# Single-unit expert loads put ahead of the two-unit loads, and the last rows transposed inside the down product before them, in a one-core fp32 decoder layer

## The chip, the cores and the metric

One core of one Trainium2 chip runs the whole program. The metric is the device time in microseconds (us) of one execution, as the median of several; lower is better.

## The reference, cut to what matters

A pre-norm decoder layer on x of 8 x 112 rows of 512 (896 rows): causal attention with 16 heads of 128, cross attention with 32 heads of 16 over 375 context rows per batch, then a mixture of experts. The change touches the last part alone:

```python
probs = softmax(x @ gate_w.T); w, sel = top_k(probs, 2); w /= w.sum()
combine = sum(one_hot(sel, 8) * w[..., None], axis=1)              # 896 x 8
out = silu(x @ shared_gate.T) * (x @ shared_up.T) @ shared_down.T   # inner size 704
y = einsum('nei,ehi->neh', silu(g) * u, expert_down)               # 8 experts, inner size 352
out = out + einsum('neh,ne->nh', y, combine)
x = x + out
```

## The kernel before, in words

The rows that go to one expert are gathered into slots of 128, called units. 21 units always suffice for 896 x 2 choices over 8 experts, and so 21 are computed (`NBLK`, L23). An expert's weights are loaded either for two units (kind "p", seven such loads) or for one (kind "o", seven). The list `jobs` (L324) holds the order of the loads: three shared ones ("s", numbers k = 0 to 2), then p, o, p, o ... to number 16. `its` (L326 to L335) is the list of the steps: one per shared load and one per unit, so 3 + 21. Two weight buffers exist of each kind: `F` (as loaded, fp32) and `E` (its split into a high and a low part, fp32r); load k uses number k % 2.

Each product in fp32 is made of three matmuls on high and low parts (`mm3`, L511). So each loaded weight has to be split: ScalarE writes the high part (`part_hi`, L1234), VectorE subtracts to get the low part (`part_low`, L1645). A routed load is split in four pieces: 0, 1 and 2 for the up and gate weights, 3 for the down weights. `splits(n, when)` (L376 to L387) says which pieces are split in step n: `when` 0 is at the step's start, 1 is at its end. In the pattern of before, pieces 0 to 2 of a two-unit load are split in the step of the one-unit load ahead of it, and pieces 0 to 2 of a one-unit load in the first of the two steps of the two-unit load ahead of it. For the first routed load (k = 3) all three pieces of load 4 come at the end of the step (L386).

TensorE's step for a unit (`job_pe`, L874) is: gate product of unit j (`expert_up(j, 0)`, 12 matmuls), transpose of the previous unit's hidden rows (`turn_h`, 3), transpose of the next unit's rows (`turn_x`, 4), up product (`expert_up(j, 1)`, 12), down product of the previous unit (`job_down`, 9). In the first routed step the down product of the last shared load stands second, and none stands at the end. `expert_up` waits for all three up pieces of its load. After the last step come `turn_h` and `job_down` of the last unit, unit 20 (L958, L959).

VectorE's step (`job_dve`, L1677) is: the splits of `when` 0, the low part of the previous unit's transposed hidden rows (`ht_low_dve`), the low part of the next unit's transposed rows, the product silu(g) * u (L1710), the splits of `when` 1, and `y_out` of the previous unit: its down product times the routing weight, from PSUM to `yg` (L1667). ScalarE goes in the same order (`job_act`, L1266), with the high part of the hidden rows (`ht_hi_act`) and the silu. Each engine works in the order in which its program stands.

GpSimd adds each unit's rows to the output in HBM with an indirect DMA (`add_back`, L2005). Units of one load have no row in common. Units of different loads can have, and so `add_back` waits until all adds of the load before have landed, but not for an add of its own load (L2009 to L2012).

SyncE issues the loads. `part_load(k, 0)` brings the up and gate weights (1408 KB), `part_load(k, 3)` the down weights (768 KB); each waits until VectorE has split the same pieces of load k - 2. The loop at L2174 sets the order of the queue, with one `xg_load` (the rows of the unit four later) per step.

Of the kernel before, what the change touches and what calls it, by code (L numbers as in the profile page):

```python
# [12 lines left out]
NB, T, D, NT = 8, 112, 512, 896  # L13
# [9 lines left out]
NBLK = (2 * NT + NE * (BS - 1)) // BS  # L23
NP, NO = 7, 7
NSL = NP + NO
RW = D + 2
IC = ((0, 128), (128, 128), (256, 96))
WU = KC * 2 * NI
# [52 lines left out]
def decoder_layer(nc, x_d, ctx_d, wqk_d, wv_d, wo_d, wqx_d, wkv_d, gw_d, moe_d, wexp_d, ident_d, mask_d, cst_d,  # L81
                  out_d):
    stack = ExitStack()
    with stack:
# [131 lines left out]
        o = wide + WE * 4  # L216
# [3 lines left out]
        o = end_a  # L220
# [6 lines left out]
        o = place_w + 2 * SC * 4  # L227
# [29 lines left out]
        small, o, o2 = {}, start_p, wide + WE * 4 + 2 * SC * 4  # L257
# [28 lines left out]
        for n, u in enumerate(pj_uses):  # L286
            if n == pj_turn:
                kb_last = pj_last[0], pj_last[1]
            i = n % 4 + (2 if n >= pj_turn else 0) if n + 1 < len(pj_uses) else 6
# [28 lines left out]
        for n, u in enumerate(tx_uses):  # L318
            i = 3 if n >= tx_turn else 7
# [1 line left out]
        KB, SX, AB = banks[0:2], banks[2:6], banks[6]  # L321


        jobs = [("s", j) for j in range(3)] + [(kd, q) for q in range(NP) for kd in "po"]  # L324
        NJ = len(jobs)
        its, unit_of, job_of, last_of = [], [], [], {}  # L326
        for k, (kd, q) in enumerate(jobs):
# [21 lines left out]
        for n, (kind, j, k, _) in enumerate(its):  # L349
            prev = its[n - 1] if n else None  # L350
# [17 lines left out]
        for n, u in enumerate(ups):  # L368
            i = gb[n]
# [6 lines left out]
        def splits(n, when):  # L376

            kind, j, k, second = its[n]
            if kind == "s":
                return ([(1, 0), (1, 3)], [(2, 0), (2, 3)], {0: [(3, 0)], 2: [(3, 1), (3, 2)], 1: [(3, 3)]}.get(when))[k] if when == 2 or k == 2 else []  # L380
            if when == 2 or k == NJ - 1 and not second:
                return []
            if second:
                return ([(k, 3)] if k > 3 else [], [(k + 1, 3)])[when]
            if k == 3:
                return [(4, 0), (4, 1), (4, 2)] if when else []  # L386
            return ([(k + 1, 0), (k + 1, 1)], [(k + 1, 2)])[when]  # L387
# [14 lines left out]
        for b in range(NB):  # L402
            r, row_parts[b] = 0, []
            while r < T:
                j, p = (b * T + r) // 128, (b * T + r) % 128
# [102 lines left out]
        def tensor(e):  # L508
# [96 lines left out]
            for j in range(NA + 2):  # L605
                if 1 <= j <= NA:
                    i = j - 1
# [217 lines left out]
            def turn_h(j):  # L825
                u = ("h", j)
                w.wait_ge(*gu_dve["b", j])
                t_wait(u)
                for k, (o, n) in enumerate(IC):
                    i = e.transpose(TB[u][0:n, k * 128:(k + 1) * 128], (hh1 if j % 2 else hh[0])[:, o:o + n], ident[:, :])  # L830
                i.then_inc(*t_full.did(u))
# [16 lines left out]
                else:  # L848
                    w.wait_ge(*y_done[v])

            def job_down(kind, j):
                k = job_of[j] if kind == "e" else at_job[kind, j]
                p = E[k % 2]
                if kind == "e":
                    u = (kind, j)
                    part_wait(k, 3)
                    w.wait_ge(*ht_lo[j])
                    y_wait(u)
                    for i, (o, n) in enumerate(IC):
                        z = WU + i * D  # L860
                        t = mm3(YB[u][:, :], (hT[j % 2][0][0:n, i, :], hT[j % 2][1][0:n, i, :]),
                                (p[0][0:n, z:z + D], p[1][0:n, z:z + D]), i == 0, i == 2)
                    t.then_inc(*y_full.did(u))
                    return
                w.wait_ge(*h_lo[1, 2 * j + 1])
                for t in range(4):
                    u = (kind, j, t)
                    y_wait(u)
                    for q in range(2):
                        i = mm3(YB[u][0:T, :], at(hs1 if q else hs[0], ALL, toks(t * T, T)), at(p, ALL, toks((WU if q else 0) + 1024, D)),  # L870
                                q == 0, q == 1)
                    i.then_inc(*y_full.did(u))

            def job_pe(n):  # L874
                kind, j, k, _ = its[n]
                prev = its[n - 1][0:2] if n else None
                nxt = its[n + 1] if n + 1 < len(its) else (None, 0)
                if kind == "e":
                    expert_up(j, 0)
                else:  # L880
                    up_pe(1, 2 * j, 0)
                if prev and prev[0] == "e":
                    turn_h(prev[1])
                elif prev and kind == "e":
                    job_down(*prev)
                if kind == "s":
                    up_pe(1, 2 * j, 1)
                    if k == 0:
                        up_pe(1, 2 * j + 1, 0)
                if nxt[0] == "e":  # L890
                    turn_x(nxt[1])
                if kind == "e":
                    expert_up(j, 1)
                if prev and (prev[0] == "e" or kind == "s"):
                    job_down(*prev)
                if kind == "s":
                    if k:
                        up_pe(1, 2 * j + 1, 0)
                    up_pe(1, 2 * j + 1, 1)
# [55 lines left out]

            for n in range(len(its)):
                job_pe(n)
            turn_h(NBLK - 1)  # L958
            job_down("e", NBLK - 1)  # L959


# [401 lines left out]
        def vector(e):  # L1363
# [91 lines left out]
            for j in range(NA + 2):  # L1455
# [7 lines left out]
                if 1 <= j <= NA:  # L1463
                    i = j - 1
# [191 lines left out]
            def ht_low_dve(j):  # L1656
                w.wait_ge(*ht_hi[j])
                low(hT[j % 2][1][:, :, :], TB["h", j][:, 0:3 * BS].rearrange("p (k t) -> p k t", k=3), hT[j % 2][0][:, :, :]).then_inc(
                    *ht_lo.did(j))

            def y_out(kind, j):
                if kind == "e":
                    w.wait_ge(*y_full[kind, j])
                    w.wait_ge(*meta_in[0])
                    if j > 3:
                        w.wait_ge(*added[j % 4][j - 4])
                    e.tensor_scalar(yg[j % 4][:, :], YB[kind, j][:, :], meta[:, unit_of[j], 1:2], None, ALU.mult).then_inc(  # L1667
                        *y_done.did((kind, j)))
                    return
                for t in range(4):  # L1670
                    u = (kind, j, t)
                    w.wait_ge(*y_full[u])
                    if j:
                        w.wait_ge(*y_done[kind, j - 1, t])
                    e.tensor_tensor(xs[:, 4 + t, :], xs[:, 4 + t, :], YB[u][0:T, :], ALU.add).then_inc(*y_done.did(u))

            def job_dve(n):  # L1677
                kind, j, k, _ = its[n]
                prev = its[n - 1] if n else (None, 0)
                nxt = its[n + 1] if n + 1 < len(its) else (None, 0)  # L1680
                if kind == "s":
                    up_mul(1, 2 * j)
                    for i in splits(n, 0):
                        part_low(*i)
                    if k:
                        y_out(*prev[0:2])
                    up_low(1, 2 * j)
                    if nxt[0] == "e":
                        turned_low(nxt[1])
                    for i in splits(n, 2):  # L1690
                        part_low(*i)
                    up_mul(1, 2 * j + 1)
                    up_low(1, 2 * j + 1)
                    for i in splits(n, 1):
                        part_low(*i)
                    return
                if prev[0] == "s":
                    y_out(*prev[0:2])
                for i in splits(n, 0):
                    part_low(*i)  # L1700
                if prev[0] == "e":
                    ht_low_dve(prev[1])
                if nxt[0] == "e":
                    turned_low(nxt[1])
                if j > 1:
                    w.wait_ge(*t_full["h", j - 2])
                u = ("b", j, 1)
                w.wait_ge(*gu_act["b", j])
                w.wait_ge(*gu_full[u])
                e.tensor_tensor((hh1 if j % 2 else hh[0])[:, 0:NI], (sg1 if j % 2 else sg[0])[:, 0:NI], GU[u][:, 0:NI],  # L1710
                                ALU.mult).then_inc(*gu_dve.did(("b", j)))
                for i in splits(n, 1):
                    part_low(*i)
                if prev[0] == "e":
                    y_out(*prev[0:2])

            def wqx_low(k):
# [186 lines left out]
            for n in range(len(its)):  # L1904
                job_dve(n)
            ht_low_dve(NBLK - 1)
            y_out("e", NBLK - 1)


# [115 lines left out]
        def sync(e):  # L2025
# [146 lines left out]
            part_load(4, 0)  # L2172
            part_load(4, 3)
            for kind, j, k, second in its[3:]:  # L2174
                if jobs[k][0] == "p":
                    part_load(k + 3 if second else k + 2, 0)
                else:
                    part_load(k + 1, 3)
                    part_load(k + 2, 3)
                xg_load(j + 4)  # L2180
                if j == 0:
                    for b in range(4, NB):
                        store(b)
# [67 lines left out]
```

## Time and profile before

| what | value |
| --- | --- |
| median of 3 runs | 963.21 us (962.73 to 963.60) |
| the profiled execution's own time | 963.22 us |
| its span in the trace | 961.4 us |
| TensorE busy | 928.0 us, 97% of the span |
| VectorE, ScalarE, GpSimd busy | 544.2, 455.5, 178.3 us |
| DMA | 94.12 MB, 98 GB/s over the span |

How to read it: PE is TensorE, PEld its weight load, DVE VectorE, ACT ScalarE, POOL GpSimd, SP SyncE (SPq its queue). Rows give microseconds from the start of the span. Time before the span and behind it is 1.8 us in the profiled execution. "L1367" is the line of the helper that makes every low part, "L966" the one that makes every high part, "L512" to "L514" are the three matmuls of `mm3`, "L830" is `turn_h` and "L822" `turn_x`.

### The profile page before, as it was taken

How to read it: one execution, taken by the hardware profiler on the slowest of the kernel's cores; microseconds unless marked ns; L12 is line 12 of the kernel's file. 1: busy time of each engine (PE TensorE's matmuls, PEld its weight loads, DVE VectorE, ACT ScalarE, POOL GpSimd, SP SyncE). 2: the span in 40 equal slices, each digit the busy share in tenths (PEclk: the TensorE clock that was granted, in tenths of full speed). 3: DMA queues.
4: the chain of work that ended last, by engine and by line, in shares of the span. 5: the costliest groups of instructions: out<-in, count | busy, mean ns of one | idle time of the engine just before them, and what ended most of it. 6: DMA issues, size and time to landing. Idle time of an engine off the chain costs nothing.

```text
span 961.4 us, 17906 instructions
## 1 busy us (share of the span) xinstructions
PE 928.0 (97%) x7250; PEld 807.5 (84%) x7250; DVE 544.2 (57%) x1192; ACT 455.5 (47%) x1113; POOL 178.3 (19%) x137
## 2 busy tenths in 40 slices
PE   4999999999999999999999999999999999999995
PEld 3999999999999999877777777777778888999994
DVE  6254444444444445485645546555457766888882
ACT  3342323232323233446666666566575234665651
POOL 1220202020202022411011011011000710223232
PEclk9999999999999999999999999999999999999998
DMA  5210442020202003212110010010032685998973
GB/s 190 67 45 22 166 164 66 24 66 22 66 23 67 22 22 110 65 47 88 55 34 23 13 34 23 13 33 13 1 125 80 231 247 185 335 301 280 303 198 44
DMA packets 31329, 94.12 MB, mean 98 GB/s; under 512 B 6176, under 2 KB 9488, under 8 KB 29328
## 3 DMA queue, kind: packets, MB, share of 16 engines
q1 hardware_dynamic: 26944, 83.80, 25.6%
q0 software_dynamic: 4304, 9.19, 4.7%
q8 instruction: 57, 0.93, 0.4%
q14 instruction: 24, 0.20, 0.1%
HBM read 74.33 MB, written 16.81 MB: 95 GB/s over the span
## 4 chain that ended last, share of the span: by engine, by line
PE 90%; DVE 5%; ACT 2%; issue 1%; DMA 1%; SPq 0%; POOL 0%; DVEq 0%
PE bank L512 25%; PE bank L513 24%; PE bank L514 24%; PE bank L709 3%; PE bank L726 3%; PE bank L559 3%; PE bank L584 3%; PE bank L676 1%; PE bank L571 1%; PE bank L822 1%; PE bank L736 1%; PE bank L600 1%; PE bank L830 1%; DMA wqk_f<-wqk 1%; DVE kT L1528 1%
## 5 line engine op out<-in xcount | busy, mean ns | idle before, releaser
L1130 ACT ACTIVATE ee<-bank 125x448 f32<-125x448 f32 x192 | 91.0, 547 | 22.0 <-PE bank L709 21.0
L512 PE MATMUL bank<-xT_hi,wqk_hi 128*128 128x448 f32 x256 | 95.9, 375 | 1.4 <-DVE xT_lo L1367 1.4
L514 PE MATMUL bank<-xT_lo,wqk_hi 128*128 128x448 f32 x256 | 93.8, 366 | 0.0
L513 PE MATMUL bank<-xT_hi,wqk_lo 128*128 128x448 f32 x256 | 93.6, 365 | 0.0
L512 PE MATMUL bank<-wkv_hi,ctx_hi 128*125 128x512 f32 x192 | 80.3, 418 | 2.6 <-DVE kn L1519 2.0
L1367 DVE TENSOR_TENSOR E_lo<-F,E_hi 128x940 fp32r<-128x940 f32 (+2 forms) x62 | 81.0, 1330 | 2.4 <-ACT E_hi L966 2.3
L513 PE MATMUL bank<-wkv_hi,ctx_lo 128*125 128x512 f32 x192 | 76.1, 396 | 0.0
L514 PE MATMUL bank<-wkv_lo,ctx_hi 128*125 128x512 f32 x192 | 75.7, 394 | 0.0
L512 PE MATMUL bank<-wv_hi,xT_hi 128*112 128x256 f32 x256 | 72.2, 282 | 0.0
L513 PE MATMUL bank<-wv_hi,xT_lo 128*112 128x256 f32 x256 | 71.8, 280 | 0.0
L514 PE MATMUL bank<-wv_lo,xT_hi 128*112 128x256 f32 x256 | 71.7, 280 | 0.0
L1914 POOL TENSOR_TENSOR ctx_lo<-ctx_f,ctx_hi 128x500 fp32r<-128x500 f32 x24 | 30.4, 1267 | 220.4 <-ACT ctx_hi L966 220.4
L1449 DVE TENSOR_TENSOR xa<-xa,bank 128x512 f32<-128x512 f32 x56 | 38.4, 686 | 53.1 <-PE bank L514 53.1
L966 ACT ACTIVATE E_hi<-F 128x940 fp32r<-128x940 f32 (+2 forms) x62 | 68.0, 1146 | 0.9
L1528 DVE COPY kT<-bank 128x250 f32<-128x250 f32 x48 | 20.0, 418 | 84.8 <-PE bank L676 84.7
L2016 POOL DMA_INDIRECT out<-yg,meta x21 | 38.8, 1849 | 142.9 <-DVE yg L1667 76.8
L1914 POOL TENSOR_TENSOR wqk_lo<-wqk_f,wqk_hi 128x1024 fp32r<-128x1024 f32 x16 | 37.8, 2362 | 145.4 <-ACT wqk_hi L966 145.4
L966 ACT ACTIVATE qk<-bank 128x448 f32<-128x448 f32 x32 | 17.4, 545 | 96.1 <-PE bank L514 96.1
L1025 ACT ACTIVATE pp<-sm,nm 112x112 f32<-112x112 f32 x128 | 48.0, 377 | 30.7 <-DVE nm L1421 30.7
L512 PE MATMUL bank<-E_hi,xgT_hi 128*128 128x352 f32 x168 | 56.3, 335 | 0.0
L1110 ACT ACTIVATE sq<-bank 125x256 f32<-125x256 f32 (+1 forms) x64 | 24.6, 384 | 64.6 <-PE bank L514 64.6
L514 PE MATMUL bank<-E_lo,xgT_hi 128*128 128x352 f32 x168 | 54.2, 322 | 0.0
(323 smaller groups left out, 2401.0 us busy)
## 6 DMA issues: line engine op xcount, KB each, us to landing
F<-wexp SPq DMA_DIRECT2D x14, 1408.0 KB, 7.4
F<-wexp SPq DMA_DIRECT2D x14, 768.0 KB
wqk_f<-wqk SPq DMA_DIRECT2D x16, 512.0 KB, 3.4
ctx_f<-ctx SPq DMA_DIRECT2D x24, 250.0 KB, 2.7
slots<-zt SPq DMA_DIRECT2D x1, 5397.0 KB, 19.0
xg<-slots SPq DMA_DIRECT2D x21, 256.0 KB, 7.0
F<-moe SPq DMA_DIRECT2D x6, 768.0 KB, 6.8
wv_f<-wv SPq DMA_DIRECT2D x8, 512.0 KB, 3.6
```

The costliest lines, as they stand in the source:

```text
L512: e.matmul(out, a[0], b[0], start=first, stop=False)
L513: e.matmul(out, a[1], b[0], start=False, stop=False)
L514: return e.matmul(out, a[0], b[1], start=False, stop=last)
L559: i = e.matmul(banks[4 + g][0:T, c * T:(c + 1) * T], q[:, 0, toks(b * T, T)], q[:, 1, toks(b * T, T)], start=True, stop=True)
L966: return e.activation(out, src, ACT.Copy)
L1025: i = e.activation(pp[g][:, c, :], sm[g][:, c, :], ACT.Exp, bias=nm[g][:, c:c + 1], scale=ISQ, accum_out=rs[g][:, c:c + 1])
L1130: e.activation(ee[(4 * n + r) % 8][:, :], SX[r][0:MS, 0:4 * T], ACT.Exp, scale=0.25).then_inc(*x_exped.did((n, r)))
L1367: return e.tensor_tensor(out, src, high.bitcast(F32), ALU.subtract)
L1449: e.tensor_tensor(xa[:, j, :], xa[:, j, :], PJ[u][:, :], ALU.add).then_inc(*pj_dve.did(u))
L1528: e.tensor_copy(kT[n % 6][:, :, :], TX["t", (u, m)][:, 0:2 * MS].rearrange("p (g t) -> p g t", g=2)).then_inc(*k_copied.did((u, m)))
L1914: return e.tensor_tensor(out, src, high.bitcast(F32), ALU.subtract)
L2016: e.indirect_dma_start(out_d, bass.IndirectOffsetOnAxis(ap=meta[:, unit_of[j], 0:1].bitcast(U32), axis=0), yg[j % 4][:, :], None, compute_ ...
```

## The change

The list of loads alternates o, p instead of p, o. So the routed loads begin with a one-unit load (k = 3) and end with a two-unit load (k = 16); unit numbers and the work per unit stay. `splits` and SyncE's order of loads follow. The last step now makes the first third of unit 19's down product, transposes unit 20's hidden rows, and then makes the other two thirds. `y_out` of unit 19 goes behind the low part of unit 20's hidden rows.

```diff
-        jobs = [("s", j) for j in range(3)] + [(kd, q) for q in range(NP) for kd in "po"]
+        jobs = [("s", j) for j in range(3)] + [(kd, q) for q in range(NP) for kd in "op"]
...
             if second:
-                return ([(k, 3)] if k > 3 else [], [(k + 1, 3)])[when]
+                return ([(k, 3)], [(k + 1, 3)] if k + 1 < NJ else [])[when]
             if k == 3:
                 return [(4, 0), (4, 1), (4, 2)] if when else []
...
-            def job_down(kind, j):
+            def job_down(kind, j, inner=range(3)):
...
-                    for i, (o, n) in enumerate(IC):
-                        z = WU + i * D
+                    for i in inner:
+                        n, z = IC[i][1], WU + i * D
                         t = mm3(YB[u][:, :], (hT[j % 2][0][0:n, i, :], hT[j % 2][1][0:n, i, :]),
                                 (p[0][0:n, z:z + D], p[1][0:n, z:z + D]), i == 0, i == 2)
-                    t.then_inc(*y_full.did(u))
+                    if i == 2:
+                        t.then_inc(*y_full.did(u))
...
-                if prev and (prev[0] == "e" or kind == "s"):
+                if n == len(its) - 1:
+                    job_down(*prev, (0,))
+                    turn_h(j)
+                    job_down(*prev, (1, 2))
+                elif prev and (prev[0] == "e" or kind == "s"):
                     job_down(*prev)
...
             for n in range(len(its)):
                 job_pe(n)
-            turn_h(NBLK - 1)
             job_down("e", NBLK - 1)
...
-                if prev[0] == "e":
+                if prev[0] == "e" and n + 1 < len(its):
                     y_out(*prev[0:2])
...
             ht_low_dve(NBLK - 1)
+            y_out("e", NBLK - 2)
             y_out("e", NBLK - 1)
...
             for kind, j, k, second in its[3:]:
-                if jobs[k][0] == "p":
-                    part_load(k + 3 if second else k + 2, 0)
-                else:
-                    part_load(k + 1, 3)
+                if k == 3 or jobs[k][0] == "p" and not second:
+                    part_load(k + 2, 0)
+                if second:
+                    part_load(k + 2, 3)
+                    part_load(k + 3, 0)
+                elif jobs[k][0] == "o":
                     part_load(k + 2, 3)
                 xg_load(j + 4)
```

## Rows read from the trace of the kernel before

**Rows 1.** The page: chain of work that ended last, shares by engine.

```profile
PE 90%; DVE 5%; ACT 2%; issue 1%; DMA 1%; SPq 0%; POOL 0%; DVEq 0%
```

**Rows 2.** Busy time in stretches: us, each engine's busy time, granted clock, DMA share, GB/s.

```profile
783.00:812.00 29.00, 28.79 (x141) 24.27 (x140) 18.64 (x23) 10.94 (x16) 0.00 (x0) 1.00 0.69 225
812.60:945.00 132.40, 132.40 (x791) 123.37 (x790) 109.48 (x131) 79.22 (x111) 35.74 (x19) 1.00 0.83 261
```

**Rows 3.** Timeline, first routed step's end: start, duration, engine, line, tiles, [idle before].

```profile
811.74 2.74 ACT L966 ACTIVATE E_hi<-F 128x940 fp32r<-128x940 f32 x3
...
812.52 0.33 PE L514 MATMUL bank<-E_lo,xgT_hi 128*128 128x352 f32 x1
...
812.69 0.32 PE L512 MATMUL bank<-E_hi,xgT_hi 128*128 128x352 f32 x1
...
812.96 0.52 DVE L1710 TENSOR_TENSOR sg<-sg,bank 128x352 f32<-128x352 f32 x1 [0.73 <-PE bank L514]
...
813.39 3.22 DVE L1367 TENSOR_TENSOR E_lo<-F,E_hi 128x940 fp32r<-128x940 f32 x3
```

**Rows 4.** The chain of waits, a wait of TensorE for VectorE: start, duration, what.

```profile
806.68 0.69 DVE xs L1675
...
807.42 0.49 PE bank L512
```

**Rows 5.** Timeline, around the end of a later one-unit step.

```profile
925.56 1.13 DVE L1367 TENSOR_TENSOR E_lo<-F,E_hi 128x936 fp32r<-128x936 f32 x1
...
926.87 0.19 PEld L512 LDWEIGHTS bank<-E_hi,xgT_hi 128*128 128x128 f32 x1 [0.21 <-DVE E_lo L1367]
```

**Rows 6.** Timeline, the last step and what follows it.

```profile
944.54 0.39 PE L512 MATMUL bank<-E_hi,hT1hi 128*128 128x512 f32 x1
...
944.84 0.52 DVE L1710 TENSOR_TENSOR sg<-sg,bank 128x352 f32<-128x352 f32 x1 [0.92 <-PE bank L514]
...
946.63 0.49 PE L830 MATMUL bank<-ident,sg 128*128 128x128 f32 x3
946.83 0.75 DVE L1667 TENSOR_SCALAR yg<-bank,meta 128x512 f32<-128x512 f32 x1 [1.46 <-PE bank L514]
947.15 0.49 ACT L966 ACTIVATE hT0hi<-bank 128x384 fp32r<-128x384 f32 x1 [3.46 <-PE bank L830]
947.68 0.56 DVE L1367 TENSOR_TENSOR hT0lo<-bank,hT0hi 128x384 fp32r<-128x384 f32 x1
947.86 1.55 POOL L2016 DMA_INDIRECT out<-yg,meta  x1 [4.61 <-DVE yg L1667]
...
948.34 0.47 PE L512 MATMUL bank<-E_hi,hT0hi 128*128 128x512 f32 x1 [1.22 <-issue]
...
950.28 0.40 PE L514 MATMUL bank<-E_lo,hT0hi 96*128 96x512 f32 x1
950.72 0.75 DVE L1667 TENSOR_SCALAR yg<-bank,meta 128x512 f32<-128x512 f32 x1 [2.48 <-PE bank L514]
953.24 1.55 POOL L2016 DMA_INDIRECT out<-yg,meta  x1 [3.83 <-issue]
```

**Rows 7.** DMA issues of the stretch 946 to 961.4: tiles, count, median us to landing.

```profile
out<-yg,meta POOLq DMA_INDIRECT x2, 4.7
```

**Rows 8.** Busy time in a stretch behind the last matmul, columns as in rows 2.

```profile
954.00:955.00 1.00, 0.00 (x0) 0.00 (x0) 0.00 (x0) 0.00 (x0) 0.78 (x1) 0.72 0.00 0
```

**Rows 9.** Timeline, near the start: the same matmul at both levels of the clock.

```profile
18.64 0.72 PE L512 MATMUL bank<-xT_hi,wqk_hi 128*128 128x448 f32 x1
...
22.52 0.41 PE L513 MATMUL bank<-xT_hi,wqk_lo 128*128 128x448 f32 x1
```

**Rows 10.** Landing of the 28 issues of line 2141 (the routed loads): one line.

```profile
DMA to landing us min/median/max: 6.1/7.4/9.3
```

**Rows 11.** Timeline, SyncE's issues over a two-unit load's steps.

```profile
873.72 0.34 SPq L2141 DMA_DIRECT2D F<-wexp  x1
...
876.52 5.27 SPq L2141 DMA_DIRECT2D F<-wexp  x2
```

## The prediction

> **What bounds the kernel now.** I read the page's chain of waits first: TensorE holds 90% of it, "issue" 1%, DMA 1% [rows 1]. Then the busy time by stretch: from 812.6 to 945 us, which is all of the routed part but its first step and its last two microseconds of steps, TensorE is busy 132.40 of 132.40 us at the full granted clock, with 791 matmuls [rows 2]. A unit takes 40 matmuls (12 + 12 + 9, and 7 transposes), so a step lasts 132.4 x 40 / 791 = 6.7 us, and no wait of another engine shows in it. In the stretch before (783 to 812) TensorE lacks 0.2 us. So a reordering of the loads can't gain anything in the middle: 21 units make the same matmuls in either order. It can only open a gap where there was none, or close something at the two ends. The timeline of both ends therefore decides.
>
> **The end, before.** Unit 19's down product begins at 944.54; nine matmuls later, at 946.63, so 0.23 us for each, the transposes of unit 20 follow, ScalarE's high part starts at 947.15, VectorE's low part at 947.68, and the last down product at 948.34: TensorE idles 1.22 us. Its last matmul starts at 950.28, VectorE scales from 950.72 to 951.47, but GpSimd issues the last add only at 953.24, 3.83 us idle, since it waits for the add of 947.86 to land [rows 6]. From that issue to the end of the span are 961.4 - 953.2 = 8.2 us.
>
> **The change, part by part.** The sum is made against the profiled execution, 963.22 us, which is also the median (963.21).
>
> 1. *First routed step.* This is the part that costs. Load 4 is now needed one step earlier, since load 3 serves one unit and not two. Its three up pieces are still split at the end of step 3, behind the product silu(g) * u, and TensorE has nothing left there: the down product of the shared load stood second in that step. The rows show the whole chain. The last matmul of the step starts at 812.52, and the next unit's first at 812.69. VectorE makes the product at 812.96 and the three low parts from 813.39 on, 3.22 us in all, to 816.61; ScalarE's high parts run from 811.74 to 814.48, ahead of them [rows 3]. From a VectorE end to the matmul it releases 0.05 us pass (807.37 to 807.42) [rows 4]. So unit 1's gate product starts at 816.65 instead of 812.69: 3.96 us. The first matmul after a gap takes 0.1 to 0.25 us more (0.49 us long where others take 0.40 [rows 4]); I take 0.1. **Cost 4.1 us**, 3.9 to 4.3. Nothing takes it back, since TensorE has no later idle time to absorb it [rows 2].
>
> 2. *Later steps of one-unit loads.* There too the next load's third up piece is split at the end of the step, and the next unit needs it at once, but the down product of the previous unit covers it. The trace has this pattern six times already: the low part starts at 925.56 and takes 1.13 us, to 926.69, and TensorE's next weight load comes at 926.87 [rows 5]. Its cover is only some 0.2 us longer than it. Cost 0 as the pattern stays the same; without cover it would be up to 1.1 us each.
>
> 3. *First step of the two-unit loads, and the move of the piece-3 splits.* As many ScalarE and VectorE instructions as before, in the same kinds of steps; VectorE is busy 109.5 of 132.4 us, ScalarE 79.2 [rows 2]. In the new last step VectorE has one piece more at its start: 1536 elements where 940 take 1.07 us [rows 3], so 1.8 us. `ht_low` can't start there before the gate product's 12 matmuls, 0.17 us each [rows 3], and the transposes are done, over 2.5 us in. Cost 0.
>
> 4. *SyncE's queue.* 28 loads as before. The up part of a one-unit load now goes out behind the down part of the load ahead, so at about 876.9 instead of 873.72 [rows 11], and behind 768 KB. Two steps of 13.4 us lay between its issue and the first step that splits it; 10.2 us are left. Landing takes 6.1 to 9.3 us, median 7.4 [rows 10]; 768 KB at 261 GB/s [rows 2] are 3.0 us, but part of that is in these landings already. TensorE needs those pieces a further step later, so that only a delay of ScalarE's and VectorE's queue could matter. Cost 0, with an upper end below. `xg_load` goes out a step late at most and is needed three steps on: 0.
>
> 5. *Unit 20's transposes inside unit 19's down product.* A third of the down product, 3 x 0.23 us, ends at 945.24. `turn_h` waits for VectorE's product, 944.84 + 0.52, so it starts at about 945.45 and TensorE idles 0.2 us. The high part, low part and down product follow 0.52, 1.05 and 1.71 us behind, as before [rows 6]: 947.17. The three transposes and six matmuls fill TensorE until then. So the last down product starts 948.34 - 947.17 = 1.2 us earlier. Its scaled rows are there at 951.47 - 1.17 = 950.30, and GpSimd can issue 0.28 us later (947.58 to 947.86): 950.58.
>
> 6. *No wait between the last two adds.* `y_out` of unit 19 comes after its six later matmuls, at 947.36 to 948.10, and its add at 948.38, with 1.55 us of work, so to 949.93 [rows 6]. The last add's 950.58 is later than that, so it goes out at once, 2.66 us before the old 953.24. An add alone takes 4.7 us to land [rows 7]. Add 19 must now wait for add 18, of another load, but a whole step of 6.7 us lies between the two, and 4.7 us is what landing takes. **Gain 2.7 us** with part 5. If the two adds, 2.2 us apart, got in each other's way wholly, the second would be as if it had waited, and the end would come at 948.38 + (953.24 - 947.86) = 953.76 instead of 953.24: a loss of 0.5 us. Nearest row is the lone add; I take 2.7.
>
> Sum: 963.2 + 4.1 - 2.7 = **964.6 us**, 0.15% above before. A measurement of this kernel can tell about 0.2% from no change, so 961.3 to 965.1 counts as the same. The forecast's own range is 964.1 to 965.3.
>
> **The rivals.**
>
> *A, slower: the gap lowers TensorE's clock.* The new gap is 4.0 us long, longer than any that TensorE has while at full clock. At the end of the run the granted clock is 0.72 on average over 954 to 955 [rows 8], with levels 1.0 and 0.5, so it fell at about 954.4, 3.8 us after the last matmul ended. Near the start, ten 448-column matmuls go out from 18.64 to 22.52, 0.39 us apart, before one takes 0.41 us instead of 0.72 [rows 9]: that stretch ran at half clock. At the full one 352 columns follow after 0.17 us (812.52 to 812.69) [rows 3], which is 0.22 for 448. So a fall would cost such a stretch once, 3.9 x (1 - 0.22/0.39) = 1.7 us, and up to twice that if it stays longer: 966.3, up to 968.0. For it: the lengths are almost equal. Against it: the matmuls on either side are dense. The Trainium skill ("TensorE: Matmul & The Clock Gate", HAM oscillation) says that idle stretches between bursts of matmuls send the clock back to half rate; by that rule the time is this rival's, without it the forecast's. The fall at the end of the trace agrees, but the trace has no such gap with matmuls behind it.
>
> *B, slower: the last add gains little.* If the second add's data queue behind the first's, the end gives between -0.5 and 1.2 us: 963.2 + 4.1 + 0.5 = 967.8 down to 966.1. For it: both go through one queue. Against: 2.2 us lie between the issues, and an add takes 4.7 us from issue to landing, most of it a delay that can overlap.
>
> *C, slower: loads come late.* It decides when landing takes more than about 10.2 us. 9.3 + 3.0 = 12.3 us would be 2.1 us late, six times at most: 12.6 us. For it: DMA is busy 83% in this stretch [rows 2]. Against: no wait of ScalarE for a load is among the idle times, and the first 1 to 2 us would be absorbed. A likely size is 0 to 2 us in all, 964.6 to 966.6.
>
> *D, faster: the gap at the start isn't there.* If unit 1's weights were ready in time, only the end would count: 963.2 - 2.7 = 960.5. For it: ScalarE is done by 814.5 and loads are early. Against: VectorE's program has the product ahead of the low parts, and that waits for the up product of the same step. As the code stands the gap must come.
>
> **How the numbers follow.** Forecast 0.60; A 0.17; B 0.10; C 0.07; D 0.06. The range 963.6 to 967.0 holds the forecast, most of A, half of B and of C, which is about 0.8 to 0.85. Faster: D and a little, 0.07. Slower: A, B, most of C and a fifth of the forecast, 0.17 + 0.10 + 0.05 + 0.12 = 0.44. Same: the rest, 0.49.
>
> **What would show it.** In the changed profile, TensorE should have one idle time of about 4 us some 813 us into the span, ended by VectorE's L1367 on E_lo, and then none to the last step. There the transposes of the last unit should stand after three matmuls of the down product, the idle time of 1.22 us should be gone but for 0.2, and GpSimd's last two issues stand 2.2 us apart, the last about 8.2 us from the end. A is right if the matmuls after the gap stand 0.32 us or so apart; B if the last issue is early but the span's end isn't; C if ScalarE waits for DMA. The forecast is wrong if the gap is under 3 us, or if more gaps show after it.

## The result and the profile after

| kernel | median us | lowest to highest | ratio to before, 95% interval |
| --- | --- | --- | --- |
| before | 963.40 (6 runs) | 962.73 to 964.47 | |
| changed | 966.90 (6 runs) | 966.24 to 968.42 | 1.0038 [1.0025, 1.0051] |

The change makes the kernel 0.38% slower, 3.5 us by the medians. Its profiled execution took 966.24 us, with a span of 964.4 us, 3.0 us longer than before's. TensorE again holds 90% of the chain. Beside the experiments below, before was timed again, 27 times (median 963.40) with the first four kernels and 20 times (963.01) on another chip with the last four; two of the 27 executions, of 1675.59 and 3199.4 us, are left out of every ratio.

The idle times of TensorE behind the first 700 us, by what ended them. The first line is new; the second was there before.

```profile
PE bank L512 <- DVE E_lo L1371: 4.0, 1, 4.0
...
PE bank L600 <- DVE qT L1540: 0.3, 1, 0.3
```

That is the forecast gap, once and of the forecast length. The timeline around it (start, duration, engine, line, tiles, idle before) answers to [rows 3]:

```profile
811.17 4.49 ACT L970 ACTIVATE E_hi<-F 128x940 fp32r<-128x940 f32 x5
...
811.96 0.32 PE L514 MATMUL bank<-E_lo,xgT_hi 128*128 128x352 f32 x1
812.39 0.52 DVE L1714 TENSOR_TENSOR sg<-sg,bank 128x352 f32<-128x352 f32 x1 [0.73 <-PE bank L514]
812.83 5.32 DVE L1371 TENSOR_TENSOR E_lo<-F,E_hi 128x940 fp32r<-128x940 f32 x5
816.26 0.63 PE L512 MATMUL bank<-E_hi,xgT_hi 128*128 128x352 f32 x1 [3.98 <-DVE E_lo L1371]
816.69 0.49 PE L513 MATMUL bank<-E_hi,xgT_lo 128*128 128x352 f32 x1
816.98 0.49 PE L514 MATMUL bank<-E_lo,xgT_hi 128*128 128x352 f32 x1
...
819.62 0.36 PE L514 MATMUL bank<-E_lo,xgT_hi 128*128 128x352 f32 x1
819.82 0.49 PE L830 MATMUL bank<-ident,sg 128*128 128x128 f32 x3
```

Everything here stands 0.6 us earlier than in the trace of before. TensorE's stop and VectorE's chain are as worked out: VectorE's row of five low parts holds load 4's three and two of later pieces. From the last matmul to unit 1's first are 4.30 us where before's had 0.17. New is what follows the gap: the matmuls stand 0.29 us apart (816.69 to 816.98) where the same ones stood 0.17 us apart at the end of the step before, and they take 0.49 us where they took 0.32. The gate product's 12 matmuls last from 816.26 to 819.82, 3.56 us, where before's lasted 1.93, from 812.69 to the transposes:

```profile
814.62 0.49 PE L830 MATMUL bank<-ident,sg 128*128 128x128 f32 x3
```

That is 1.6 us more. The busy time by stretch shows the granted clock (the figure behind POOL's):

```profile
812.00:818.00 6.00, 2.02 (x8) 1.77 (x7) 5.61 (x6) 3.66 (x5) 0.00 (x0) 0.86 0.49 168
818.00:825.00 7.00, 7.00 (x39) 6.56 (x38) 3.14 (x6) 3.64 (x5) 0.00 (x0) 0.88 0.58 227
825.00:830.00 5.00, 5.00 (x34) 4.85 (x33) 3.96 (x6) 2.94 (x5) 2.88 (x1) 1.00 0.28 27
830.00:948.00 118.00, 118.00 (x703) 109.69 (x701) 95.74 (x115) 68.00 (x95) 32.46 (x18) 1.00 0.90 269
```

The level reads 1.00 (2.4 GHz) up to 816 and 0.50 (1.2 GHz) from 816.5 to 817. So 0.86 over 6 us and 0.88 over 7 us are 6 x 0.14 / 0.5 + 7 x 0.12 / 0.5 = 3.4 us at half clock, from where the gap ends. From 830 to 948 TensorE is busy throughout, as in [rows 2].

The end, answering to [rows 6]:

```profile
949.96 0.39 PE L512 MATMUL bank<-E_hi,hT1hi 128*128 128x512 f32 x1
...
950.83 0.55 PE L830 MATMUL bank<-ident,sg 128*128 128x128 f32 x3
951.14 0.48 PE L512 MATMUL bank<-E_hi,hT1hi 128*128 128x512 f32 x1
...
954.52 0.40 PE L514 MATMUL bank<-E_lo,hT0hi 96*128 96x512 f32 x1
...
954.96 0.75 DVE L1671 TENSOR_SCALAR yg<-bank,meta 128x512 f32<-128x512 f32 x1 [1.40 <-PE bank L514]
...
953.84 1.55 POOL L2021 DMA_INDIRECT out<-yg,meta  x1 [4.02 <-DVE yg L1671]
955.99 1.55 POOL L2021 DMA_INDIRECT out<-yg,meta  x1 [0.60 <-DVE yg L1671]
```

From the start of unit 19's down product, the last matmul comes after 954.52 - 949.96 = 4.56 us instead of 5.74 (944.54 to 950.28), 1.2 us sooner, and the last add after 6.03 us instead of 8.70 (944.54 to 953.24), 2.7 us sooner. Both are the forecast numbers. From the last issue to the end of the span it is 8.4 us instead of 8.2, so 2.4 us remain.

The account in spans: gap 4.0, half clock 1.6, end -2.4, all else -0.2; 3.0 us together. The last term comes by subtraction, and it holds the 0.6 us by which this trace was ahead before the changed part began; the changed part alone costs 3.6 us, close to the 3.5 by the medians.

### The profile page after: what moved, and what is told of

It is laid out like the page before. It is cut to its first block, busy times and chain, and to the rows that moved or that the text cites. A ratio compares the mean times of both kernels' runs of the same rounds, so it can differ in the third digit from the quotient of the medians.

```text
span 964.4 us, 17902 instructions
## 1 busy us (share of the span) xinstructions
PE 929.4 (96%) x7250; PEld 808.7 (84%) x7250; DVE 544.4 (56%) x1192; ACT 455.1 (47%) x1113; POOL 180.1 (19%) x137
## 4 chain that ended last, share of the span: by engine, by line
PE 90%; DVE 5%; ACT 2%; issue 1%; DMA 1%; SPq 0%; POOL 0%; DVEq 0%
PE bank L512 25%; PE bank L513 24%; PE bank L514 24%; PE bank L709 3%; PE bank L726 3%; PE bank L559 3%; PE bank L584 3%; PE bank L676 1%; PE bank L571 1%; PE bank L822 1%; PE bank L736 1%; PE bank L600 1%; PE bank L830 1%; DMA wqk_f<-wqk 1%; DVE kT L1532 1%
## 5 line engine op out<-in xcount | busy, mean ns | idle before, releaser
L970 ACT ACTIVATE E_hi<-F 128x940 fp32r<-128x940 f32 (+2 forms) x62 | 67.8, 1147 | 10.0 <-DMA F<-wexp 10.0
L970 ACT ACTIVATE qk<-bank 128x448 f32<-128x448 f32 x32 | 17.4, 544 | 96.2 <-PE bank L514 96.2
L513 PE MATMUL bank<-E_hi,xgT_lo 128*128 128x352 f32 x168 | 54.8, 326 | 0.0
```

Of the source, the lines that this page charges most:

```text
L513: e.matmul(out, a[1], b[0], start=False, stop=False)
L970: return e.activation(out, src, ACT.Copy)
```

## The experiments

Every kernel below was timed in turn with the kernel before on the same chip; ratios are to before. The changed kernel itself was timed beside the last three only (its second median, 966.37 us, is from there). A cut is marked with "...".

**Is it the clock?** The wait of the changed kernel stays, but TensorE gets work for it, on data that has long been ready, and the result is overwritten by the next product:

```diff
                 elif prev and (prev[0] == "e" or kind == "s"):
                     job_down(*prev)
+                if n == 3:
+                    gu_wait(("b", j + 1, 0))
+                    for _ in range(22):
+                        e.matmul(GU["b", j + 1, 0][:, 0:NI], xT[0][:, 0, 0:128], xT[0][:, 1, 0:NI], start=True, stop=True)
```

> The changed kernel with 22 matmuls of 352 columns more, whose result is overwritten, put on TensorE in the gap at the start of the second routed step; their operands have long been ready. They take about 22 x 0.16 = 3.5 us of the 4.0 us gap, so the wait for VectorE's low parts stays and only TensorE's idleness goes. Theory (the idle gap lowers the clock, and the half clock behind it costs 1.6 us in the trace, and twice that in some executions): the matmuls behind the gap stand 0.16 us apart, no stretch shows a clock under 1.00, and the time is 1.6 to 2.5 us under the changed kernel, so about 964.6 to 965.2, 1.3 to 1.8 us over before. Rival (the clock fell for another reason, or the late low parts alone cost all of it): no change, about 966.9.

Measured: 964.80 us, ratio 1.0017 [1.0008, 1.0027], 2.1 us under the changed kernel's first median and 1.6 under its second (966.37, below). Its 11 executions lie from 964.07 to 966.06, the changed kernel's 11 from 965.93 to 968.42. Its timeline around the same place:

```profile
812.05 3.70 PE L904 MATMUL bank<-xT_hi 128*128 128x352 f32 x22
816.24 0.40 PE L512 MATMUL bank<-E_hi,xgT_hi 128*128 128x352 f32 x1 [0.48 <-DVE E_lo L1375]
816.47 0.33 PE L513 MATMUL bank<-E_hi,xgT_lo 128*128 128x352 f32 x1
816.64 0.32 PE L514 MATMUL bank<-E_lo,xgT_hi 128*128 128x352 f32 x1
816.79 0.32 PE L512 MATMUL bank<-E_hi,xgT_hi 128*128 128x352 f32 x1
```

Unit 1's gate product starts at the same moment as in the changed kernel (816.24, 816.26), behind the same VectorE work, but its matmuls stand 0.16 us apart, and every stretch from 812 to 940 has a granted clock of 1.00. So the clock fell because TensorE was idle, and a useless filling gives that part back. This also splits the cost: the wait costs about 4 us whatever TensorE does in it (4.35 us from the last matmul of unit 0 to the first of unit 1, where before has 0.17), the clock 1.6 to 2.1.

**The order alone**, with the tail of before (unit 20's transposes behind unit 19's down product, `y_out` of unit 19 ahead of the low part); the edit is against the changed kernel:

```diff
-                if n == len(its) - 1:
-                    job_down(*prev, (0,))
-                    turn_h(j)
-                    job_down(*prev, (1, 2))
-                elif prev and (prev[0] == "e" or kind == "s"):
+                if prev and (prev[0] == "e" or kind == "s"):
                     job_down(*prev)
...
+            turn_h(NBLK - 1)
             job_down("e", NBLK - 1)
...
-                if prev[0] == "e" and n + 1 < len(its):
+                if prev[0] == "e":
                     y_out(*prev[0:2])
...
-            y_out("e", NBLK - 2)
             y_out("e", NBLK - 1)
```

> The changed order of loads, with the old tail: unit 20's transposes behind the whole down product of unit 19, and y_out of unit 19 ahead of the low part. Theory: the start costs as much as in the changed kernel (4.1 us gap, 1.6 us or more of half clock), TensorE idles 1.2 us before the last down product again, and the last add goes out 0.3 us after its y_out, at 951.75 where before had 953.24, so the end gains 1.5 us where the whole change gains 2.4. Time about 1.0 us over the changed kernel, 967.9. Rival (the adds get in each other's way when issued close together): with the adds 3.9 us apart instead of 2.2 the end comes as early as in the changed kernel, 966.9.

Measured: 968.63 us, ratio 1.0059 [1.0045, 1.0073], 1.7 us over the changed kernel's first median and 2.3 over its second; only 5 runs, with single ones from 966.95 to 969.19, so the size is rough (1.0 was expected). VectorE's last scaling and GpSimd's last two issues:

```profile
955.67 0.75 DVE L1668 TENSOR_SCALAR yg<-bank,meta 128x512 f32<-128x512 f32 x1 [2.46 <-PE bank L514]
```

```profile
953.10 1.55 POOL L2017 DMA_INDIRECT out<-yg,meta  x1 [3.71 <-DVE yg L1668]
956.70 1.55 POOL L2017 DMA_INDIRECT out<-yg,meta  x1 [2.05 <-DVE yg L1668]
```

The add goes out 0.28 us behind VectorE's end (956.42), without waiting for the one of 953.10: the order does what it is for. From the last matmul to the last issue it is 1.46 us instead of before's 2.96, so the order gains 1.5 us there, and its start costs what the changed kernel's does (a gap of 4.0 us, then 3.5 us at half clock). The 8.4 us from the last issue to the end of the span (965.1) are the same with the adds 3.6 us apart as with 2.15, so nothing here speaks for adds that get in each other's way.

**The tail alone**, with the order of before; the edit is against the kernel before:

```diff
-                if prev and (prev[0] == "e" or kind == "s"):
+                if n == len(its) - 1:
+                    job_down(*prev, (0,))
+                    turn_h(j)
+                    job_down(*prev, (1, 2))
+                elif prev and (prev[0] == "e" or kind == "s"):
                     job_down(*prev)
...
-            turn_h(NBLK - 1)
             job_down("e", NBLK - 1)
...
-                if prev[0] == "e":
+                if prev[0] == "e" and n + 1 < len(its):
                     y_out(*prev[0:2])
...
+            y_out("e", NBLK - 2)
             y_out("e", NBLK - 1)
```

> The kernel before with the change of the tail alone: unit 20's transposes inside unit 19's down product, y_out of unit 19 behind the low part. The order of loads is that of before. Theory: the last down product starts 1.2 us earlier, but the last add must wait for the one before it to land, and that one goes out 0.5 us later than before, so the end comes 0.5 us later: 963.9, no gain at all, the last issue 5.4 us behind the one before it. Rival (TensorE's end sets the end): 1.2 us faster, 962.2.

Measured: 963.77 us, ratio 1.0008 [0.9999, 1.0017]: no gain, 0.4 us over before by the medians, with an interval that just holds no change. The last two adds:

```profile
948.66 1.55 POOL L2021 DMA_INDIRECT out<-yg,meta  x1 [3.69 <-DVE yg L1671]
954.10 1.55 POOL L2021 DMA_INDIRECT out<-yg,meta  x1 [3.88 <-issue]
```

VectorE had scaled the last rows by 950.55, but the add waited until 954.10, 5.4 us behind the other, as forecast. From there to the end of the span (962.6) it is 8.5 us, so the 8.4 of the changed kernel aren't a price of two adds in flight. So the 1.2 us that TensorE gains at the end is worth nothing as long as the last two adds belong to different loads. The two halves of the change need each other: by the time of the last issue the order is worth 1.5 us, the tail alone nothing, both 2.7 us (2.4 by the end of the span).

**Load 4's pieces split early.** Piece 2 lies where the shared load has nothing, and piece 0 only where the first half of its up weights is; neither has to wait for its down product. Their low parts go between the adds of the shared load's rows, piece 1's ahead of silu(g) * u (ScalarE's high part likewise, not shown):

```diff
             if k == 3:
-                return [(4, 0), (4, 1), (4, 2)] if when else []
+                return ([(4, 0), (4, 2)], [], [(4, 1)])[when]
...
-                            if kind == "s" and k == 3 and p == 0:
+                            if kind == "s" and (k == 3 and p == 0 or k == 4 and p != 1):
                                 w.wait_ge(*gu_full["u", 1, 2 * j, 1])
...
                     e.tensor_tensor(xs[:, 4 + t, :], xs[:, 4 + t, :], YB[u][0:T, :], ALU.add).then_inc(*y_done.did(u))
+                    if j == 2 and t in (1, 2) and t - 1 < len(splits(3, 0)):
+                        part_low(*splits(3, 0)[t - 1])
...
-                for i in splits(n, 0):
+                for i in splits(n, 0) if n > 3 else []:
                     part_low(*i)
...
                     turned_low(nxt[1])
+                for i in splits(n, 2):
+                    part_low(*i)
```

> The changed kernel with load 4's up pieces split earlier: pieces 0 and 2 while the last shared load's down product runs (VectorE's low parts between the second, third and fourth of its adds), piece 1 ahead of silu(g) * u. Theory: unit 1's gate product starts about 0.7 to 1.2 us late instead of 4.0, the clock doesn't fall, and the end keeps its gain of 2.4 us. Time about 4.9 us under the changed kernel: 962.0, 1.4 us under before. Rival (the pieces put early delay the shared load's adds or the product, and the gap comes back there): gap plus new waits of 2 us or more, time 963.5 or above.

Measured: 962.21 us, ratio 0.9991 [0.9982, 1.0001], 4.2 to 4.7 us under the changed kernel; against before the interval just holds no change. One wait is left there, at the full clock:

```profile
813.38 0.40 PE L512 MATMUL bank<-E_hi,xgT_hi 128*128 128x352 f32 x1 [0.88 <-DVE E_lo L1373]
```

**One piece early**, the other two as in the change, for a gap between the two lengths; the rest of the edit is as in the experiment above:

```diff
             if k == 3:
-                return [(4, 0), (4, 1), (4, 2)] if when else []
+                return ([(4, 2)], [(4, 0), (4, 1)], [])[when]
```

> The changed kernel with one piece (piece 2) of load 4 split early, the other two still behind silu(g) * u. Theory of the parts: the gap is one low part shorter, 4.0 - 1.1 = 2.9 us. If the clock falls only behind the full 4 us gap, the matmuls behind it stand 0.16 us apart and the time is 1.1 + 1.6 to 2.5 us under the changed kernel, about 964.0. If it falls behind a gap of 2.9 us too, the time is only 1.1 us under the changed kernel, about 965.8.

Measured: 964.44 us, ratio 1.0014 [1.0005, 1.0023]. The median is near the first number, but the 11 runs are not alike: nine lie from 963.23 to 964.92, two at 966.00 and 966.42. The profiled execution is the one of 966.00:

```profile
815.11 0.40 PE L512 MATMUL bank<-E_hi,xgT_hi 128*128 128x352 f32 x1 [2.83 <-DVE E_lo L1373]
815.34 0.32 PE L513 MATMUL bank<-E_hi,xgT_lo 128*128 128x352 f32 x1
...
816.72 0.49 PE L512 MATMUL bank<-E_hi,xgT_hi 128*128 128x352 f32 x1
...
819.68 0.43 PE L514 MATMUL bank<-E_lo,xgT_hi 128*128 128x352 f32 x1
819.95 0.32 PE L512 MATMUL bank<-E_hi,xgT_hi 128*128 128x352 f32 x1
```

Here a gap of 2.8 us was enough, and the matmuls run 1.4 us at the full clock (from 815.11, 0.16 us apart) before they slow down, for 3.4 us. In how many of the other ten executions the clock fell isn't known: none was profiled, and before alone spreads over 2.6 us in the same runs (961.73 to 964.35). The profiled execution also lost 0.6 us elsewhere, to a load that came late. ScalarE waited 3.62 us for weights, the hidden rows' low part stood behind them in VectorE's queue, and TensorE waited for it:

```profile
899.19 1.87 ACT L970 ACTIVATE E_hi<-F 128x940 fp32r<-128x940 f32 x2 [3.62 <-DMA F<-wexp]
...
902.92 0.51 PE L512 MATMUL bank<-E_hi,hT0hi 128*128 128x512 f32 x1 [0.56 <-DVE hT0lo L1373]
```

**No gap left.** As the kernel with load 4's pieces split early, and unit 1's row transposes ahead of the shared load's down product, so that VectorE can make their low part and piece 1's before the last of the four adds:

```diff
                 elif prev and kind == "e":
+                    turn_x(nxt[1])
                     job_down(*prev)
...
-                if nxt[0] == "e":
+                if nxt[0] == "e" and n != 3:
                     turn_x(nxt[1])
...
+                    if j == 2 and t == 2:
+                        turned_low(1)
+                        part_low(4, 1)
```

> As the kernel with the pieces split early, and also unit 1's row transposes ahead of the shared load's down product, so that VectorE makes their low part and piece 1's before the last of its four adds. Theory: the gap of 1.0 us left there closes to under 0.3, and the time is 0.8 us under it, about 961.4, 2.0 under before. Rival (VectorE is now full there and the last add or the product delays TensorE elsewhere): a new wait at the transposes of unit 0 or the second down product, time 962.2 or more.

Measured: 961.00 us, ratio 0.9973 [0.9962, 0.9984]: 0.27% faster than before, and clear of it. VectorE's queue in that stretch is now nearly full, and TensorE's wait there is 0.39 us (under 0.3 was expected):

```profile
809.80 1.12 DVE L1374 TENSOR_TENSOR E_lo<-F,E_hi 128x936 fp32r<-128x936 f32 x1
810.85 0.68 DVE L1374 TENSOR_TENSOR xgT_lo<-bank,xgT_hi 128x512 fp32r<-128x512 f32 x1
811.58 1.14 DVE L1374 TENSOR_TENSOR E_lo<-F,E_hi 128x940 fp32r<-128x940 f32 x1
812.64 0.68 DVE L1682 TENSOR_TENSOR xs<-xs,bank 112x512 f32<-112x512 f32 x1
```

```profile
812.82 0.40 PE L512 MATMUL bank<-E_hi,xgT_hi 128*128 128x352 f32 x1 [0.39 <-DVE E_lo L1374]
```

**The loads' order in SyncE's queue.** The profile of the changed kernel has ScalarE wait for loads, which the profile of before doesn't show: "ACT E_hi L970 <- DMA F<-wexp: 10.0, 5, 2.2" (10.0 us in five waits, the longest 2.2).

```diff
                 if second:
-                    part_load(k + 2, 3)
                     part_load(k + 3, 0)
+                    part_load(k + 2, 3)
```

> The changed kernel with SyncE's two issues of a two-unit load's second step the other way round: the up part of the one-unit load ahead of the down part. Theory: ScalarE's five waits for a load (10 us in all, up to 2.2 us each in the changed kernel) shrink or go, but they were hidden, so the time stays within 0.5 us of the changed kernel, 966.9. Rival (the late loads cost some of the 3.5 us): 1 us or more under it.

Measured: 966.28 us, ratio 1.0033 [1.0022, 1.0043], beside 966.37 for the changed kernel in the same runs. The five waits are gone from its list and the time is the same: they were hidden. (The one wait of TensorE behind such a late load in all profiles is the 0.6 us of the kernel with one piece early.) Its profiled execution, 967.69 us, happens to show a longer stretch at half clock:

```profile
812.00:818.00 6.00, 1.99 (x10) 1.72 (x9) 5.27 (x7) 4.41 (x6) 0.00 (x0) 0.78 0.53 197
818.00:824.00 6.00, 6.00 (x28) 5.92 (x28) 2.14 (x3) 2.09 (x4) 0.00 (x0) 0.65 0.77 284
```

That is 6 x 0.22 / 0.5 + 6 x 0.35 / 0.5 = 6.8 us at half clock, twice the stretch of the changed kernel's profile, with the same gap of 4.0 us. But it began at 815.4, within the gap, and matmuls ran again only from 817.04, so 5.2 us of it held work. From unit 1's first matmul to its up product are 5.00 us here (817.04 to 822.04), 4.24 in the changed kernel's profile (816.26 to 820.50) and 2.61 in before (812.69 to 815.30): a loss of 2.4 us instead of 1.6. That explains some 0.8 of the 1.8 us between this execution and the changed kernel's of 965.93; the rest, 1.0 us, had gone by before the gap (the last matmul ahead of it stands at 812.70 here and at 811.73 there).

**The changed kernel again**, in the same runs as the last three.

> The changed kernel once more, on the chip of these runs: theory and rivals alike 966.9, with single executions from 966.2 to 968.5 as the half-clock stretch is met once or twice.

Measured: 966.37 us, ratio 1.0039 [1.0025, 1.0052], single executions from 965.93 to 968.29. The result stands. In this profile the clock fell 0.8 us after the matmuls behind the gap had begun (816.03 to about 816.86), again for 3.4 us.

## Why the prediction was wrong

The predicted time of 964.6 us called the change a draw with before. It was 966.9 us: just inside the wide range (963.6 to 967.0), outside the forecast's own (964.1 to 965.3), and clearly slower than before. Point by point:

1. *The first routed step* was forecast to start unit 1 3.96 us late, at a cost of 4.1. It starts 4.13 us late (4.30 us between the two matmuls instead of 0.17), and TensorE idles 3.98. The chain that sets it (the product, then three low parts behind it in VectorE's queue) is the one described. Right.
2. *Later one-unit steps, the two-unit steps* cost 0. TensorE is busy for 118 of 118 us behind 830. Right.
3. *SyncE's queue* was given 0 with an upper end in which loads come late. They do come late for ScalarE, by up to 2.2 us in the changed kernel's profile, and cost nothing there, as the swapped queue shows. Right in price, though with little to spare: in the kernel with one piece early a wait of 3.6 us reached TensorE and cost 0.6. The argument "no wait of ScalarE for a load" came from before and no longer held.
4. *The end* was forecast at 2.7 us, and measured 2.4. The last add went out 2.7 us sooner, but then 8.4 instead of 8.2 us passed; what makes up those 0.2 us wasn't found, and the tail alone has them too (over all ten profiles this stretch takes 8.2 to 8.8 us, before's being the shortest). That neither half would bring its sum alone is shown by the tail alone, which gains nothing.
5. *The clock is the step that failed.* The sum priced the gap at its length alone and put the fall of the clock at 0 beside it, as rival A with a chance of 0.17. The fall was the likely case: it is in both profiles of the changed kernel, in that of the order alone and in that of the swapped queue, and every execution of the changed kernel lies at 965.9 us or above, where 964.8 is the median with the gap filled. Its price of 1.7 us was right: the traces of the changed kernel lose 1.6, and forecast and rival together give 966.3. "Up to twice that" was not met: the longest stretch at half clock in a trace is indeed twice as long, but lost 2.4 us, since part of it lay in the gap. The price also rested on [rows 9] as a stretch at half clock; the granted clock in before's trace reads 1.00 there (15 to 24 us), and nine of the ten matmuls take 0.57 us, only the first 0.72, so that row alone didn't show the level. The changed kernel's matmuls bear it out: 0.29 us for 352 columns at half clock is 0.37 for 448, the distance of those nine. What made me hold it unlikely was that the matmuls on either side are dense. The profile with one piece early shows that density behind the gap doesn't save the clock: it fell 1.4 us after they had begun again. The row that should have decided was [rows 8]: a fall 3.8 us behind the last matmul, against a new gap of 4.0. The delay isn't a fixed one, though: in the swapped queue's profile the fall came 2.4 us after the last matmul had ended (813.0 to 815.4).

The Trainium skill ("TensorE: Matmul & The Clock Gate", HAM oscillation) says that idle stretches between bursts of matmuls send the clock to half rate. The traces agree: 3.4 us at half clock behind a 4.0 us gap in the changed kernel, and none when the gap is filled.

Rival B (adds in each other's way) is refuted by the last adds of three kernels, 2.15, 3.6 and 5.4 us apart and all 8.4 to 8.5 us from the end, C (late loads) for the changed kernel by the swapped queue, and D (no gap) by the trace.

## What to carry to other kernels

When an order of work is turned round to gain at its end, look at what its start now needs one step sooner, and whether that step has cover. Price a new gap of several microseconds on TensorE at its length plus a stretch at half clock, and if the gap can't be closed, even useless matmuls in it give the second part back. A wait that an engine program imposes by its order (three splits behind a product that nobody was yet waiting for) was here cheaper to mend than to trade: with the splits and unit 1's transposes moved, the same change is 2.0 us faster than before (961.00 against 963.01 in the same runs) instead of 3.5 slower.

## What the runs showed of the hardware that was not expected

- A gap of 2.8 us between dense matmuls was enough for the clock to fall in a profiled execution, and it fell only 1.4 us after TensorE had work again. The other ten executions weren't profiled.
- The same gap of 4.0 us goes with 3.4 us at half clock in one execution and with 6.8 in another (the changed kernel's profiles and the swapped queue's). The fall came 2.4 us into the gap in the swapped queue's, as matmuls began again in the changed kernel's first, and 0.8 us later than that in its second.
- The transposes run slower too while the clock is half: seven of them took from 817.60 to 818.94 us in the kernel with one piece early, 1.3 us, where 0.7 is usual (814.62 to 815.30 in before).
